# Float32 messages read by their upper halves, and the target marks of a sweep turned to 8 bits by transfers from GpSimd

## The reference

```python
x = _layernorm(x + _L0_gnn_ref(x, src, dst))                      # sum of x[src] at dst
x = _layernorm(x + _L1_gnn_ref(x, edge_attr_32, eps, W1, b1, W2, b2, edge_index))
x = _layernorm(x + _L2_gnn_ref(x, src, dst, edge_weight, weight))
x = _layernorm(x + _L3_gnn_ref(x, edge_index, w_src, w_tgt, gate_bias))
# L2: rows = src, cols = dst
gathered = x[cols] * vals[:, None]
z = segment_sum(gathered, rows);  return z @ weight
# L3: out degree of src, a gate per edge
norm = deg_inv_sqrt[src] * deg_inv_sqrt[dst]
gate = sigmoid(x[src] @ w_src + x[dst] @ w_tgt + gate_bias[0])
out = segment_sum((norm * gate)[:, None] * x[src], dst)
```

## Time and profile before

| | |
|---|---|
| runs | 7746.34, 7761.68, 7761.24 us; median 7761.24 |
| span of the profiled execution | 7749.5 us (nothing else is given for what lies around it) |
| mean granted TensorE clock | 0.85 of full speed |
| busy: PE, PEld, DVE, ACT, POOL | 75%, 70%, 89%, 51%, 53% |
| sort and scatter, sweeps 0 and 1, their nodes | 0 to 4590 us |
| sweep q = 2 | 4590 to 6243 us |
| nodes(2) | 6243 to 6340 us |
| sweep q = 3 | 6340 to 7613 us |
| last node stage and the store of the result | 7613 to 7749.5 us |

### The profile page before, as it was taken

How to read it: one execution, slowest core, us unless ns; L and a number is a source line. 1 busy time by engine, 2 the same in 40 slices (tenths; PEclk the granted TensorE clock), 3 DMA queues, 4 the chain that set the end, 5 groups by cost and what they waited for, 6 DMA issues and landing times.

```text
span 7749.5 us, 288101 instructions
## 1 busy us (share of the span) xinstructions
PE 5814.2 (75%) x120824; PEld 5431.9 (70%) x120824; DVE 6911.0 (89%) x8082; ACT 3965.9 (51%) x5752; POOL 4139.2 (53%) x3710
## 2 busy tenths in 40 slices
PE   5777776688888567666667667787787749999995
PEld 4666665677777466666666667777777749999995
DVE  8999998999999699899999958898898879999993
ACT  2333332344444255555555538899998833333331
POOL 5777777777777777777777500000000016666661
PEclk8888888999999688888888867778777769999996
DMA  7995111677666477777777526666666636666661
GB/s 134 176 176 84 27 27 27 167 175 176 176 176 151 131 212 212 208 211 211 209 212 209 188 97 203 208 215 213 209 215 203 206 104 202 202 203 202 202 202 36
DMA packets 1123441, 1316.77 MB, mean 170 GB/s; under 512 B 581317, under 2 KB 869253, under 8 KB 1122183
## 3 DMA queue, kind: packets, MB, share of 16 engines
q1 hardware_dynamic: 768861, 739.56, 34.8%
q10 hardware_dynamic: 250536, 508.89, 22.4%
q0 software_dynamic: 103168, 54.68, 3.0%
HBM read 902.26 MB, written 400.43 MB: 168 GB/s over the span
## 4 chain that ended last, share of the span: by engine, by line
POOL 38%; PE 22%; issue 19%; DVE 8%; DMA 6%; ACT 5%; SPq 1%; DVEq 1%; ACTq 0%; POOLq 0%
POOL slot_table L675 37%; PE banks L1601 6%; PE banks L1547 6%; DMA slot_table<-recs,idx_now 5%; PE banks L1612 4%; PE banks L1635 3%; ACT far_now L1356 3%; POOL msg_z L686 2%; PE banks L1638 1%; PE banks L1482 1%; DVE hot_d L950 1%; DVE hot_d L1070 1%; DVE hot_td L969 1%; DVE left L1103 1%; SPq L429 1%
## 5 line engine op out<-in xcount | busy, mean ns | idle before, releaser
L675 POOL DMA_INDIRECT slot_table<-recs,idx_now x3224 | 3275.1, 1016 | 1020.1 <-issue 940.1
L686 POOL TENSOR_TENSOR msg_z<-left,msg_z 128x448 bf16<-128x448 f32 x364 | 814.7, 2238 | 2390.7 <-ACT msg_z L1389 2390.7
L1547 PE MATMUL banks<-hot_d,msg 128*96 128x256 bf16 x10192 | 1542.6, 306 | 711.6 <-DVE msg L1032 502.0
L1547 PEld LDWEIGHTS banks<-hot_d,msg 128*96 128x96 bf16 x10192 | 1259.3, 136 | 852.5 <-DVE msg L1032 539.7
L950 DVE TENSOR_TENSOR hot_d<-lodl,banks 128x2560 bf16<-128x2560 bf16 (+1 forms) x884 | 1485.1, 1680 | 0.0
L1356 ACT CAST far_now<-hot_td 128x3584 fp8e4<-128x3584 bf16 x364 | 1153.9, 3170 | 35.5 <-DVE hot_td L969 32.8
L1601 PE MATMUL banks<-x_win,hot_td 128*128 128x32 bf16 x30576 | 883.5, 182 | 214.9 <-issue 201.2
L1601 PEld LDWEIGHTS banks<-x_win,hot_td 128*128 128x128 bf16 x30576 | 831.4, 100 | 241.8 <-issue 227.7
L1320 ACT CAST near_now<-hot_t 128x1792 fp8e4<-128x1792 bf16 x364 | 613.4, 1685 | 702.1 <-DMA source_marks<-near_now 594.6
L1289 ACT CAST msg<-banks 128x480 bf16<-128x480 f32 (+1 forms) x1040 | 522.1, 554 | 631.5 <-PE banks L1547 593.7
L961 DVE TENSOR_TENSOR hot_t<-lo_bc,banks 128x1280 bf16<-128x1280 bf16 (+1 forms) x884 | 805.9, 912 | 11.2 <-DMA lo_bc<-row_table 11.1
(11 more groups left out here) (190 smaller groups left out, 9752.3 us busy)
## 6 DMA issues: line engine op xcount, KB each, us to landing
lo_bc<-row_table ACTq DMA_DIRECT2D x364, 448.0 KB
dl_bc<-row_table SPq DMA_DIRECT2D x364, 448.0 KB, 4.5
target_marks<-far_now SPq DMA_DIRECT2D x364, 448.0 KB, 3.0
dl_bc<-target_marks SPq DMA_DIRECT2D x364, 448.0 KB, 4.1
lo_bc<-row_table ACTq DMA_DIRECT2D x468, 320.0 KB
slot_table<-zeros SPq DMA_DIRECT2D x52, 1617.0 KB, 10.9
rec_in<-slot_table ACTq DMA_DIRECT2D x364, 231.0 KB
source_marks<-near_now ACTq DMA_DIRECT2D x364, 224.0 KB
```

Source lines behind the costliest of these rows:

```text
L675: pool.indirect_dma_start(out=slot_dram[c.number], out_offset=bass.IndirectOffsetOnAxis(ap=idx_now[:, c.slot, g:g + 1], axis=0), in_=recs[ ...
L686: pool.tensor_tensor(msg3[:, blk.slot, :, 2 * D:3 * D], left3[:, blk.slot], msg3[:, blk.slot, :, D:2 * D], ALU.subtract).then_inc(msg_made ...
L1547: mm = t.matmul(banks[0:3 * D, 6 + blk.par, 0:WIN], rows[:, blk.slot, g, :], hot[:, blk.slot, g // 2, :, g % 2], start=(blk.b == 0 and g = ...
```

## The change

Five edits, all on the fast path.

1. The messages of both late sweeps stay float32 in one tile `msg3` with three buffers. Part 1 is no longer a rounded copy: PE reads the upper 16 bits of each float32 word in place (`top3`, a bfloat16 view with a step of two elements), and DVE or GpSimd subtracts this view from the word to get the next part, also float32. ACT's four casts (L1349, L1365, L1381, L1389), `total3` and `left3` go. In q = 2 DVE makes both subtractions, one block ahead; in q = 3 DVE makes the first, one block ahead, and GpSimd the second. The column that counts edges is set to 1 once, by a memset, instead of by L1073 in each block.
2. `hot_td` gets three buffers, and the 8-bit marks are stored from it directly: GpSimd issues two transfers a block that read bfloat16 and write 8-bit floats (`store_far` on `pool`). ACT's cast L1356, `far_now` and SP's stores go; ACT has no instruction left in the sweep q = 2. DVE waits before a new `hot_td` for the two stores of three blocks ago.
3. The sweep q = 3 gets a third PSUM bank for its gathers, and its DVE loop another order. DVE's loops of both sweeps and the GpSimd ones are written out.
4. The memset of `agg3` moves from DVE in `nodes(2)` to GpSimd, behind the store of the layer-1 result and ahead of its first transfer of q = 2.
5. The store of the result is split: 112 partitions, 15 partitions, and the last one.

```diff
+WHOLE = (P - 1) // 16 * 16
-        hot_td = sb("hot_td", [P, 2, 2, BG * P], BF16, late)
+        hot_td = sb("hot_td", [P, 3, 2, BG * P], BF16, late)
-        total3 = sb("total3", [P, 2, BG, D], F32, late)
-        left3 = sb("left3", [P, 2, BG, D], F32, late)
-        msg_z = sb("msg_z", [P, 2, BG, 3 * D + 1], BF16, late)
+        msg3 = sb("msg3", [P, 3, BG, 3 * D + 1], F32, late)
+        top3 = msg3[:, :, :, :].rearrange("p s g q -> p (s g q)").bitcast(BF16).rearrange(
+            "p (s g q t) -> p s g q t", s=3, g=BG, t=2)[:, :, :, :, 1]
...
+                for first, end in ((0, WHOLE), (WHOLE, P - 1)):
+                    sp.dma_start(out[first * HB:end * HB, :].rearrange("(l h) f -> l h f", h=HB), xs[first:end, :, :]
+                                 ).then_inc(stored[3], 16)
...
+            def make_last(q, at):
                 for blk, more in straight():
-                    pool.wait_ge(second_made[3], blk.number + 1)
-                    pool.tensor_tensor(msg3[:, blk.slot, :, 2 * D:3 * D], left3[:, blk.slot],
-                                       msg3[:, blk.slot, :, D:2 * D], ALU.subtract).then_inc(msg_made[3], 1)
+                    pool.wait_ge(rest_made[q], blk.number + 1)
+                    pool.tensor_tensor(msg3[:, blk.third, :, at + D:at + 2 * D], msg3[:, blk.third, :, at:at + D],
+                                       top3[:, blk.third, :, at:at + D], ALU.subtract).then_inc(msg_made[q], 1)
+
+            def store_far():
+                for blk, more in straight():
+                    pool.wait_ge(hot_t_made[2], 2 * blk.number + 2)
+                    for k in (0, 1):
+                        pool.dma_start(
+                            far_dram[blk.chunk, blk.b, :, :].bitcast(F8)[:, k * BG * P:(k + 1) * BG * P],
+                            hot_td[:, blk.third, k, :]).then_inc(far_out[blk.third], 16)
 
             def fast():
-                sum_gated()
+                pool.wait_ge(stored[1], 16)
+                pool.memset(agg3[:, :], 0.0).then_inc(sums_cleared, 1)
+                store_far()
+                make_last(3, D)
...
-                        v.memset(agg3[:, :], 0.0)
...
-                dve.wait_ge(far_kept, 2 * blk.number + 2)
+                if blk.number >= 3:
+                    dve.wait_ge(far_out[blk.third], far_stored(blk.third, blk.number))
...
-                    s.copy(far_now[:, blk.slot, :].bitcast(F8), hot_td[:, blk.slot].rearrange("p k m -> p (k m)"),
-                           saturate=False).then_inc(far_kept, 2)
```

More of the change, by code:

```diff
@@ L59, in __init__ @@
         self.slot = place % 2
+        self.third = self.number % 3
         self.h0 = self.n * self.b
@@ L305, in build_program @@
         near_kept, near_out = sem("near_kept"), sem("near_out")
-        far_kept, far_out = sem("far_kept"), [sem(f"far_out{s}") for s in (0, 1)]
+        far_out = [sem(f"far_out{s}") for s in range(3)]
         lo_in = [sem(f"lo_in{r}") for r in range(SBPC)]
@@ L350, in landed, with far_stored @@
             return 16 * (chunks * len(range(k, G, LANES)) + more)
+        def far_stored(third, blocks):
+            return 32 * len(range(third, blocks, 3))
         def wait_scattered(eng, chunks):
@@ L579, in fast @@
                 sp.wait_ge(near_out, 16 * BLOCKS)
-                for slot in (0, 1):
-                    sp.wait_ge(far_out[slot], 16 + 16 * (BLOCKS // 2))
+                for third in range(3):
+                    sp.wait_ge(far_out[third], far_stored(third, BLOCKS))
                 load_chunk(1, 0, 0)
@@ L1036, in sum_targets @@
             def sum_targets():
+                v.memset(msg3[:, :, :, D], 1.0)
                 def take(blk):
@@ L1097, in sum_gated @@
                 make_logits(first.ahead(1))
-                for blk, more in sweep(dve):
+                subtract_first(first)
+                for blk, more in straight():
                     if more >= 1:
                         take(blk.ahead(1))
-                    dve.wait_ge(first_made[3], blk.number + 1)
-                    part = lambda q: msg3[:, blk.slot, :, q * D:(q + 1) * D]
-                    v.tensor_tensor(left3[:, blk.slot], total3[:, blk.slot], part(0), ALU.subtract
-                                    ).then_inc(rest_made[3], 1)
+                    make_hot_d(3, blk, hot_d3)
+                    if more >= 1:
+                        subtract_first(blk.ahead(1))
                     if more >= 2:
                         make_logits(blk.ahead(2))
-                    make_hot_d(3, blk, hot_d3)
                     if blk.b == 1:
                         add_sums(3, agg3, blk.chunk, 1 - blk.par, blk.number + 1)
-                    dve.wait_ge(rest_made[3], blk.number + 1)
                 add_sums(3, agg3, NCH, 1, BLOCKS + 2)
@@ L1297, in make_first @@
                     act.wait_ge(summed[1], blk.number + 1)
-                    s.activation(msg[:, blk.slot, :, 0:D], total[:, blk.slot], ACT.Relu).then_inc(first_made[1], 1)
+                    s.activation(msg[:, blk.slot, :, 0:D], total[:, blk.slot], ACT.Relu).then_inc(first_made, 1)
                 def keep_weight(blk):
@@ L1332, in sum_edges @@
                     act.wait_ge(rest_made[1], blk.number + 1)
-                    s.copy(msg[:, blk.slot, :, D:2 * D], left[:, blk.slot]).then_inc(second_made[1], 1)
+                    s.copy(msg[:, blk.slot, :, D:2 * D], left[:, blk.slot]).then_inc(second_made, 1)
                     if more >= 1:
@@ L1567, in sum_sources @@
                         gather(blk.ahead(2))
-                    sum_block(0, blk, msg, hot_d)
+                    sum_block(0, blk, msg[:, blk.slot], hot_d)
             def sum_edges():
@@ L1586, in sum_edges @@
                     pe.wait_ge(msg_made[1], blk.number + 1)
-                    sum_block(1, blk, msg, hot_d)
+                    sum_block(1, blk, msg[:, blk.slot], hot_d)
             def sum_targets():
@@ L1612, in scatter @@
                             mm = t.matmul(banks[:, blk.b, at:at + cols], hot_s[:, blk.slot, g // 2, :, g % 2],
-                                          msg_z[:, blk.slot, g, first:end], start=False, stop=False,
+                                          top3[:, blk.third, g, first:end], start=False, stop=False,
                                           skip_group_check=True)
@@ L1642, in sum_gated @@
                 first = Block(0, 0)
-                gather(first)
-                gather(first.ahead(1))
-                pe.wait_ge(taken[3], 1)
-                gather(first.ahead(2))
+                for k in range(3):
+                    gather(first.ahead(k))
                 for blk, more in straight():
                     if more >= 3:
-                        pe.wait_ge(taken[3], blk.number + 2)
+                        pe.wait_ge(taken[3], blk.number + 1)
                         gather(blk.ahead(3))
                     pe.wait_ge(msg_made[3], blk.number + 1)
-                    sum_block(3, blk, msg3, hot_d3)
+                    sum_block(3, blk, top3[:, blk.third, :, 0:3 * D], hot_d3)
             def fast():
```

121 lines of the change are left out of this document (43 added, 78 removed).

## The result

The changed kernel takes 8032.6 us (median of 4 runs, 8025.43 to 8054.55) against 7761.46 of the kernel before beside it: 1.0353 of its time, 95% interval 1.0338 to 1.0367. The change costs 271 us, where 127 were forecast. The profiled execution has a span of 8031.5 us against 7749.5, 282 more.

The account below looks back on a forecast made before the run. It took PE as the bound of q = 3, and the arrival of PE's instructions in most blocks of q = 2. Terms -54 - 9 + 64 - 20 + 146 = +127 on 7761 gave 7888 us, range 7690 to 8100.

Parts of the forecast that it names:

- Store of the result: End of the kernel: the split store spreads over 16 engines, 8 us instead of 62, -54 us.
- Memset: nodes(2) and first marks of q = 2: clearing agg3 leaves DVE but may delay its marks, -9 us.
- Sweep q = 3: Last sweep: DVE's new order waits for the gate and GpSimd, 3.66 us a block against 3.485, +64 us.
- The 3.41 of the prediction's last line: Sweep q = 3: the forecast called itself wrong if the round stays at 3.41 us.
- Sweep q = 2, what goes: Sweep q = 2: DVE loses L1073 and its waits for ACT, -20 us, bounds 0 and -80.
- a quarter: Sweep q = 2: share taken of DVE's possible gain, as instruction waits show in 296 places and DVE's in 145.
- Sweep q = 2, what comes: Sweep q = 2: load of GpSimd's converting stores makes PE's instruction packets 0.4 us later each, +146 us, bounds 0 and +330.
- The prediction's number for the rule: Sweep q = 2: a third busy queue row costs 8 descriptors a round, said to be near 0.4 us a packet.
- A: Rival for q = 2: PE's instructions come as before, last term 0, 7742 us; chance 0.25.
- C: Rival for q = 2: converting transfers or their issue are the bound, near 8570 or 8095 us; chance 0.2.
- C's second ground: Sweep q = 2: GpSimd can't issue two transfers a round while DVE works; 8095 us at 5.5 us a block.
- D: Rival: q = 3 loses nothing as PE stays the bound, q = 2 waits for DVE go; 7638 to 7700 us; chance 0.15.

Follow-up runs that it names:

- the run of the two ends: The kernel before with only the result's store split and the agg3 memset moved to GpSimd: 0.9923 of the time before.
- the two kernels with fewer instructions: Changed kernel and kernel before, each with one 96-column gather product instead of three of 32 in q = 2: 7478.1 and 7614.8 us, periods 3.839 and 4.074.

## Why the prediction was right or wrong

The direction was right, for the reason given, and the time lies in the range; the size, 127 us, was less than half of the 271 that came. That it isn't further off is in part luck: the last sweep was priced 39 us too high, against 187 too low for q = 2 with its first marks. Term by term:

- *Store of the result*, -54: measured -53.9 in the changed kernel and -53.8 alone. The reading of 4.2% as one engine at work was right. The Trainium skill ("DMA: Bandwidth & Descriptors", Why a DMA increments its semaphore by 16 and not by 1) states that the number of engines is the largest one up to 16 that divides the slowest dimension of both sides, which for 127 partitions is 1; the trace agrees, with 61 us before and 8 after.
- *Memset*, -9: -13.3 in `nodes(2)`, where the idle time ahead went too, and +4.9 at the first marks (+5.1 in the run of the two ends): -8.4. There is now a row for such a memset beside such marks: GpSimd's takes 10.77 us from 4596.19, to 4606.95, and VectorE's first mark, started at 4601.9, takes 5.56 us instead of 0.68 (min/median/max of one, first and last start):

```profile
4596.19 10.77 POOL L697 MEMSET agg<- 128x12800 f32 x1 [189.25 <-DMA x_parts<-parts]
```

```profile
L978 DVE TENSOR_SCALAR hot_td<-dl_bc,part_col x728: 666/680/5559, 4601.9 to 6553.9; 128x1792 bf16<-128x1792 bf16 x182
```

- *Sweep q = 3*, +64: measured +25. The gap behind the gate, 0.28 us, was right to the digit. Wrong was that VectorE would wait 0.13 us for GpSimd: that sum priced the subtraction at 1.01 us, from the row of before that wrote bfloat16, and had it end 0.13 late. It took 0.93 and the two overlapped by 0.07, without a loss. The value without the sharing, 3.53 us a block, was the right one (3.539). The base was a little off as well: 3.485 came from a stretch divided by its blocks, and from marks to marks the sweep has 3.464. The 3.41 of the prediction's last line has no row.
- *Sweep q = 2, what goes*, -20: some +18, on one trace each. Rows of before had shown that PE's instructions set the round, and the share of "a quarter" for VectorE's gain had no row behind it. (The 296 places of the instruction wait are 208 + 72 = 280 by the earlier trace rows.) The gain exists, 86 us in the two kernels with fewer instructions, but none of it shows while PE is late.
- *Sweep q = 2, what comes*, +146: this is the step that failed. The mechanism stands: later instructions because of the stores' load. The term was 0.4 us for each packet, from a range of 0 to 0.9. Measured is 0.81, 296 us: 0.645 for the bytes and 0.169 for GpSimd's queue. The bound of 0.9 was worked out from the backlog, a third of 2.77 us, and the middle was taken with no row for it. The bytes alone came to 0.645 of it, and the queue had no term of its own beside the load. PE's waits for "issue" went from 280 in 363 blocks to 344 in 361, so PE was late in nearly every block and nothing cushioned the delay.

The rule of the Trainium skill that the prediction weighed ("DMA: Bandwidth & Descriptors", Queues, rings and completion order), that a DMA engine goes round its queue rows and changes at packet boundaries, would put a cost on a third busy row whatever it carries. Half the bytes on GpSimd's queue against the same on SP's, 0.169 us a block, agrees with it in kind. Whether it is this rule, the writing of descriptors by GpSimd, or that on SP's queue the stores stand behind the loads instead of beside them, wasn't told apart. The prediction's number for the rule doesn't come out of its rows either: 8 rows of one transfer cost an engine 1.36 us by the earlier trace rows if the cost goes by bytes read, and 0.68 by bytes written, not near 0.4.

Of the rivals, A (no effect) and C (transfers as the bound) fell: VectorE waits 0.4 us in all for a block's stores. C's second ground, that VectorE's work would hold GpSimd's transfers back, was hardly put to the test: a block's stores start when its marks end, and only 5 of the 728 ran beside a mark (median 0.81 us against 0.53). What D said of q = 3, that PE stays the bound, holds only with the logits in their old place.

## What to carry to other kernels

Where an engine's program is written out and it waits for "issue" once in every packet of its instruction queue, count its instructions. The time that one packet of some 254 instructions needs, from asking to running, is then a bound like that of an engine, and it grew here with what other transfers moved in the same stretch. Lay the starts and ends of the queue's packets beside the stops: a fixed distance behind a packet's end tells late instructions from any other wait. A transfer that converts costs the DMA engines about what it reads, so moving this cast to the DMA engines raised the price of storing a block's marks from 1.36 us of all 16 engines, by the earlier trace rows, to 2.56 (89 x 166.10 / 16 / 361). Where such waits stand in most blocks already, nothing cushions a further delay, and no share of a gain on another engine should be counted.

## What the runs showed of the hardware

- PE's instructions come in packets of 16 KB, one for some 254 instructions. With 252 products and weight loads a block, a block takes 4.2 us with the DMA engines 36% busy (where only half of the packets come late), 4.5 at 62 to 65% on the hardware queue, 4.7 to 4.8 at 61 to 62% with GpSimd's queue in it, 5.1 at 80% on the hardware queue alone and 5.4 at 75 to 81% with GpSimd's. With 140 instructions a block the same load, 102% by its rows, delayed next to nothing.
- With 252 instructions a block, written out, PE goes on some 1.4 us (median) after the end of a packet, whatever the load, and a packet takes 0.95 to 0.96 us. What load lengthens is the time before the packet starts, 1.6 to 3.1 us after PE last went on.
- A loop of 14 blocks (3,528 instructions) is fetched on every pass, and a jump back costs 5.1 to 6.2 us; a loop of some 780 instructions ran for 1040 us without a packet.
- PE's mean granted clock over q = 2 was lower where it waited more for "issue": 0.70 with the converting stores, 0.77 before, 0.86 without stores. With fewer instructions and no such waits it was 0.97 in the changed kernel and 0.85 in the kernel before.
- GpSimd issues a direct transfer in 0.53 us (722 in 381 us), little over half of what its indirect ones take.
- A float32 memset on GpSimd held a mark of VectorE until the memset ended, 5.56 us instead of 0.68. GpSimd's subtraction takes 0.93 us and stretches VectorE's `hot_d` from 2.02 to 2.31 us when it has started first; before the change, started behind the marks, it took 2.25 us itself and they kept their 2.01.
